# Gathering pivots in pieces, and adding the base of the formed blocks on VectorE, in a frequency-domain orthogonal convolution

## The reference

```python
x = x + conv(groupnorm(x, 32 groups))           # x is 32 x 128 x 32 x 32, float32
# conv: an orthogonal convolution, made in the frequency domain (n = 34, 34 x 18 frequencies)
V = rfft2(weight, (n, n))                        # weight 128 x 127 x 3 x 3: V is 128 x 127 per frequency
W = V^H V;  W = W + eps(frequency) * I
ortho = I - 2 * V @ solve(W, V^H)                # 128 x 128 per frequency
z = irfft2(ortho @ rfft2(pad(x)))[crop] + bias
```

## Time and profile before

| | |
|---|---|
| median of 3 runs | 3013.69 us (3006.40, 3013.69, 3032.32) |
| profiled execution | 3003.69 us, of which the span from first to last instruction is 3001.9 us |
| busy share of the span | PE 87%, DVE 64%, ACT 46%, POOL 17% |
| mean granted TensorE clock | 0.888 of full speed |

### The profile page before, as it was taken

The page is one execution under the profiler, slowest core; times in us unless marked ns, Lnnn a source line. Parts: engine busy times, 40 slices in busy tenths (PEclk is TensorE's granted clock), DMA queues, the critical chain, the costliest instruction groups (busy, mean ns, idle before and its releaser), DMA issues. The chain is left out here.

```text
span 3001.9 us, 89158 instructions
## 1 busy us (share of the span) xinstructions
PE 2597.5 (87%) x38281; PEld 2135.0 (71%) x38281; DVE 1929.9 (64%) x3842; ACT 1393.9 (46%) x3398; POOL 504.8 (17%) x872
## 2 busy tenths in 40 slices
PE   4967988998998899899796787978888899959999
PEld 4945745656566778787685766757777678959999
DVE  6844506897979768568497979788788770003333
ACT  1423424434342566666553544644556546722222
POOL 0012402131310111111110111111222223410000
PEclk7978999999998999999997978979999889967777
DMA  4283484231511366474460706241232134566662
GB/s 184 85 151 69 71 164 128 85 142 45 179 38 20 61 119 130 77 156 90 98 122 13 141 14 130 52 93 55 66 102 86 56 95 127 164 132 160 162 178 93
DMA packets 562599, 310.01 MB, mean 103 GB/s; under 512 B 484616, under 2 KB 495496, under 8 KB 561368
## 3 DMA queue, kind: packets, MB, share of 16 engines
q1 hardware_dynamic: 520896, 183.58, 29.6%
q0 software_dynamic: 41312, 120.73, 12.2%
HBM read 162.85 MB, written 141.30 MB: 101 GB/s over the span
## 5 line engine op out<-in xcount | busy, mean ns | idle before, releaser
L1390 DVE SCALAR_TENSOR_TENSOR arena<-arena,psum 128x512 f32<-128x512 f32 (+2 forms) x608 | 398.9, 719 | 310.9 <-PE psum L999 310.5
L1351 DVE TENSOR_TENSOR arena<-arena 128x960 f32<-128x960 f32 (+24 forms) x480 | 399.5, 832 | 16.6
L1346 DVE TENSOR_TENSOR arena<-arena 128x960 f32<-128x960 f32 (+8 forms) x600 | 383.0, 688 | 8.2
L978 PEld LDWEIGHTS psum<-arena 32*32 32x32 f32 x9280 | 156.2, 115 | 227.4 <-issue 216.1
L999 PE MATMUL psum<-arena 32*128 32x64 f32 x9280 | 305.3, 278 | 9.8 <-ACT arena L1163 9.8
L999 PEld LDWEIGHTS psum<-arena 32*128 32x128 f32 x9280 | 284.3, 193 | 34.1 <-ACT arena L1163 20.4
L936 PE MATMUL psum<-arena 128*32 128x256 f32 (+1 forms) x2904 | 274.9, 429 | 29.6 <-DMA arena<-plain 11.2
L978 PE MATMUL psum<-arena 32*32 32x64 f32 x9280 | 182.4, 232 | 110.2 <-DVEq L1382 97.5
L940 PE MATMUL psum<-arena 128*32 128x256 f32 (+1 forms) x3696 | 276.1, 372 | 1.6 <-issue 1.6
L1142 ACT COPY arena<-arena 32x128 f32<-32x128 f32 (+3 forms) x496 | 222.0, 448 | 26.5 <-DVE arena L1390 12.4
L1045 PE MATMUL psum<-arena 128*128 128x160 f32 x1160 | 200.6, 316 | 26.3 <-ACT arena L1203 25.9
(11 more groups left out here) (121 smaller groups left out, 4860.9 us busy)
## 6 DMA issues: line engine op xcount, KB each, us to landing
blocks<-arena POOLq DMA_DIRECT2D x145, 256.0 KB, 2.5
arena<-blocks SPq DMA_DIRECT2D x290, 128.0 KB, 2.8
kept<-arena POOLq DMA_DIRECT2D x145, 256.0 KB, 3.1
arena<-kept SPq DMA_DIRECT2D x145, 256.0 KB, 2.9
xhat<-arena SPq DMA_DIRECT2D x32, 580.0 KB, 15.0
arena<-xhat SPq DMA_DIRECT2D x580, 32.0 KB, 2.6
yhat<-arena POOLq DMA_DIRECT2D x290, 64.0 KB, 2.6
arena<-x SPq DMA_DIRECT2D x8, 2048.0 KB, 10.1
```

What stands on the lines that cost most here:

```text
L978: ins = pe.matmul(psum[0][h, L * t:L * t + L], ce[h, sj % NCE, slot + t, :], M[h, home(q) + t, c, :], start=True, stop=True)
L1346: ins = dve.tensor_tensor(pr, spread(R[:, t, :, :, j], 3, 2 * w_), both, ALU.mult)
L1351: link(dve.tensor_tensor(rest, rest, pr[:, :, h], op))
L1390: ins = dve.scalar_tensor_tensor(old, old, K["mask"][:, piv:piv + 1], upd_bank(u, c)[:, 0:L * n].rearrange("p (t n) -> p t n", n=L), ALU.m ...
```

## The change

- The job `pivot b0` moves in front of `sweep a3`. Where a pivot job stands in front of a sweep of the other group (b0 before a3, a4 before b3, b4 before a7), ACT no longer gathers ahead of that sweep: it cuts the gather into pieces of one unit (8 quads, or 6 or 7; 8 pieces for group b, 11 for group a), spreads them evenly over the units of the sweep, and does each after the `copy_ju` of the following unit, where `gather_next` stands in other sweeps.
- `pivot a0` is gathered in the same pieces too, each as soon as the form units that it reads are in `M`.
- In form a, PE leaves out the matmuls for the base. DVE instead of ACT empties the bank, with one addition of the bank and the base (`tensor_tensor`, PSUM and SBUF to SBUF). Form b is as before.
- A table's tile is loaded anew only when the units that used it are in `M`, not when PE has formed them.

```diff
@@ order()
         if k == LB - 1:
-            out.append(("form", b, 0))
+            out += [("form", b, 0), ("pivot", b, 0)]
         out.append(("sweep", a, k))
-    out.append(("pivot", b, 0))
@@ SP
-                                    sp.wait_ge(S["formed" if used == "form" else "pre_done"], end)
+                                    sp.wait_ge(S["form_copied" if used == "form" else "pre_done"], end)
@@ PE: combine(), form()
-                        for p in range(LB):
+                        for p in range(LB if with_base else 0):
                             pe.matmul(columns[quadrant(p)]..., K["ident"][:, quadrant(p)],
-                                      spread(base[:, 0:m, :], 1, n), start=alone, stop=False)
+                                      spread(base[:, 0:m, :], 1, n), start=True, stop=False)
...
-                                                coefs[:, 0:m, L * p:L * p + L], start=False, stop=alone and a == n - 1)
+                                                coefs[:, 0:m, L * p:L * p + L], start=not with_base, stop=a == n - 1 or not with_base)
...
-                        combine(tile, n, QUAD * q, columns).then_inc(S["formed"], 1)
+                        combine(tile, n, QUAD * q, columns, with_base=q >= FIRST[GROUPS[1][0]]).then_inc(S["formed"], 1)
@@ ACT
                     def gather(sj, q, n):
                         act.wait_ge(S["taken"], factor_at[g, k])
+                        if k == 0:
+                            act.wait_ge(S["form_copied"], len([f for f in form_units[:formed_by[g]] if f[0] < q + n]))
+                        elif k == LB:
+                            act.wait_ge(S["s_copied"], coupled_by[g])
...
+                    def sweep_beside(at):
+                        return at + 1 < len(jobs) and jobs[at + 1][0] == "sweep" and jobs[at + 1][1] != jobs[at][1]
...
+                    def pivot_pieces(g, k):
+                        out = []
+                        for t in GROUPS[g]:
+                            q = FIRST[t]
+                            for n in UNITS_OF_SET[t]:
+                                out.append((set_job_at[g, k, t], q, n))
+                                q += n
+                        return out
...
-                            for u in range(lo, hi):
+                            for u in range(lo, hi) if g else ():
                                 copy_form(u)
...
-                            for t in GROUPS[g]:
-                                gather(set_job_at[g, k, t], FIRST[t], SLOTS_OF[t])
+                            for piece in () if sweep_beside(at) else pivot_pieces(g, k):
+                                gather(*piece)
                         elif kind == "sweep":
                             copy_u(lo)
                             copy_ju(lo)
+                            pieces_of = pivots_beside(at)
                             for u in range(lo, hi):
                                 if u + 1 < hi:
                                     copy_u(u + 1)
                                     copy_ju(u + 1)
+                                n = len(pieces_of)
+                                for sj, q, size in pieces_of[n * (u - lo) // (hi - lo):n * (u - lo + 1) // (hi - lo)]:
+                                    gather(sj, q, size)
@@ DVE, ahead of the first factoring
+                    for u in range(formed_by[0]):
+                        q, n = form_units[u]
+                        base = tiles[load_of("form", u)[4][0]][1]
+                        dve.wait_ge(S["formed"], u + 1)
+                        dve.tensor_tensor(M[:, home(q):home(q) + n, :, :],
+                                          psum[6 + u % 2][:, 0:256 * n].rearrange("p (t c n) -> p t c n", c=QUAD, n=L),
+                                          spread(base, 1, n), ALU.add).then_inc(S["form_copied"], 1)
```

More of the change, by code:

```diff
@@ L738, in build @@
         set_job_at = {(g, k, t): n for n, (g, k, t, _) in enumerate(set_jobs)}
+        formed_by = {g: max(j[4] for j in jobs if j[0:2] == ("form", g)) for g in range(len(GROUPS))}
+        coupled_by = {g: max(j[4] for j in jobs if j[0:2] == ("mid", g)) for g in range(len(GROUPS))}
         factor_at = {j: n for n, j in enumerate(FACTOR_ORDER)}
@@ L929, in _, with combine @@
                 def _(pe):
-                    def combine(tile, units, f0, columns, alone=True):
+                    def combine(tile, units, f0, columns, with_base=True):
                         coefs, base = tile
@@ L1150, in gather_next, with pivots_beside @@
                         gather(set_job_at[g, k + 1, set_jobs[sj][2]], q, n)
+                    def sweep_beside(at):
+                        return at + 1 < len(jobs) and jobs[at + 1][0] == "sweep" and jobs[at + 1][1] != jobs[at][1]
+                    def pivots_beside(at):
+                        if at == 0 or jobs[at - 1][0] != "pivot" or not sweep_beside(at - 1):
+                            return []
+                        return pivot_pieces(*jobs[at - 1][1:3])
+                    def pivot_pieces(g, k):
[6 more added lines that the diff above has]
+                        return out
                     def copy_u(u):
```

## The result

| | before | after |
|---|---|---|
| median of 4 runs each, on one chip | 3015.93 us (3006.40 to 3032.32) | 2981.91 us (2977.84 to 2990.64) |
| profiled execution | 3003.69, span 3001.9 | 2977.84, span 2976.0 |

The ratio is 0.9884, with an interval of 0.9844 to 0.9924: 35 us less, between 23 and 47. The forecast was 2987, in a range from 2968 to 3004. The number came out; two of its terms did not, and the experiments had to find out which.

What follows compares the result with a forecast made beforehand. Waits at four pivots were taken as the bound, with table 2's landing limiting form a. Terms 13.4 + 2.1 + 8.6 - 0.5 = 23.6 off 3003.69 give 2980.1; with 7 for the runs' spread, 2987, range 2968 to 3004.

Steps and rivals of the forecast that it cites:

- Form a and pivot a0, 13.4: Start of the solver: VectorE starts factoring at 463.7 instead of 477.15, 13.4 us gained, between 12.6 and 18.3.
- six low units and one full, 11.4: Form a's seven units behind table 2: six at the low clock, one at the full, 11.4 us in all.
- The price of VectorE's addition, 0.69: Form a: VectorE's addition of bank and base, not in the trace, estimated from other rows at 0.69 us.
- room: `pre a0`, TensorE's work during the first factoring: its end keeps about 5 us to spare before it is late.
- Pivot b0, 2.1: Between sweep a3 and the mid: 2.6 us from the gather leaving, less 0.5 for pieces in a3, net 2.1.
- pivot b4: Sweep a7: the gather that goes was hidden, and the eight pieces in the sweep cost 0.5 us.
- Pivot a4, 8.6: Sweep b3: first update 11.8 us earlier, less 3.2 for its pieces, net 8.6, between 7.0 and 11.8.
- the 3.2 for two doubled units: Sweep b3: two gaps between units hold two pieces; the second piece costs 1.6 us each time, 3.2 together.
- (1): Slower rival: the clock falls in the sweeps with pieces, a3, b3 and a7; 35 us lost, 3046; 4 in 100.
- The sum: Whole kernel: 13.4 + 2.1 + 8.6 - 0.5 = 23.6 us gained of the profiled execution's 3003.69, thus 2980.1.
- Rival 2: Form a: table 2 is not late, as SyncE gets through its stores sooner; whole gain 57 us, 2953; 4 in 100.
- Rival 3: Pieces cost 0.35 us in each of the 27, 9.5 instead of 4.2 lost; about 2996; 15 in 100.

Runs made afterwards that it cites:

- A repeat: The kernel after run once more, nothing edited, on another chip against the kernel before: 0.9903, median 2993.58 us.
- the experiment with table 2: Kernel after, with form a's table 2 in a tile of its own and loaded ahead of SyncE's 16 stores: 0.9868 against the kernel before.
- the kernel with the lowest ratio: Kernel after plus table 2 loaded first, one piece per gap in sweep b3, b4 gathered ahead of a7, `pre` recut: 0.9803 against before, median 2957.04 us.
- the kernel without doubled units: Kernel after, with sweep b3's pieces spread so that no two stand between the same two units: 0.9845 against the kernel before, median 2973.06 us.
- The halves: Kernel before with only the form part (form a, pivot a0): 0.9927; with only the pieces (pivots b0, a4, b4): 0.9959.
- the kernel with a doubled unit in every sweep: Kernel without sweep b3's doubled units, with two pieces put in one gap in each of twelve sweeps: 3004.93 us, a single execution.

## Why the prediction was right, and where it was not

**Form a and pivot a0, 13.4**: right in mechanism, small in size. Table 2 bounds form a and lands when it did; seven units at the mostly low clock follow. I took six low units and one full, 11.4; they took 9.2. The last hand-overs and the last piece were as sized. The transpose came 15.3 earlier counted from the span's start, and 17.4 relative to SyncE's first table DMA, since that itself was 2.2 later and the stores took 49.50 instead of 51.86. A repeat gives 16.6. Most of it is the gather's place (11.7); the lighter units give some 3 to 4. The price of VectorE's addition, 0.69, was exact. `pre a0` kept 5.80 of room, as said; the experiment with table 2 shows that little was to be won there beyond it.

**Pivot b0, 2.1**: the mid's part came as sized (third `copy_j` 11.58 behind the last update; forecast 11.4, before 14.04). What hides it is the sweep ahead. A sweep a3 or a7 takes either 39 to 42 us or 45 to 47, by how long the low clock lasts at its start: with pieces 7 long of 13, without pieces 4 long of 7. So the pieces do not choose. Within a kind, a long sweep takes some 1.8 more with them (46.92 to 47.06, against 45.00 to 45.33). In a short one the sign is open: a7 takes 40.09 to 40.23 with them and 39.08 and 39.46 without, but a3 40.34 to 41.35 with them and 41.73 without. I had said 0.5. By the long sweeps pivot b0 is worth 2.5 less 1.8, that is 0.7, and **pivot b4** -1.8 instead of -0.5, but neither is firm. The stretch from the end of sweep a3 to sweep b0's first update takes 92.1 to 92.8 in the three profiles with the gather there and 87.2 to 92.3 in the seven without. And from the end of sweep a6 to that of a7, a short a7 takes 132.9 to 133.1 with the pieces and 133.5 and 134.2 without, a long one 141.1 to 141.4 and 140.0 to 140.3: pivot b4 is between 1.4 lost and 1.3 gained. Taking b4's gather out again was part of the kernel with the lowest ratio, but not tried alone. The 5.2 of sweep a3 in the table and most of the 7.1 of sweep a7 are each a long sweep against a short one, once in after and once in before.

**Pivot a4, 8.6**: here a step failed. "Sweep b3's first update about 6 behind its first apply" held nearly (7.52; 6.46 in the kernel without doubled units), and 10.8 came back there. But the 3.2 for two doubled units measured 5.3 to 13.1 in four profiles (35.26 to 43.07, less 29.94). I had counted the wait alone, 1.6 each, and it was 1.72 and 1.79; the clock that falls behind it was in a rival of its own, (1), at 4 in 100, and there only as a fall in all three sweeps at once. It is a term of the sum: of the eighteen such waits in these runs sixteen had a fall behind them. I wrote that no row shows a fall within a sweep, and took that for evidence that there is none. The trace of the kernel before has one, in the last unit of sweep a2 (granted clock 0.50 from 874 to 875); here behind the same matmuls of sweep a0:

```profile
604.57 1.57 PE L999 MATMUL psum<-arena 32*128 32x64 f32 x48 [0.57 <-ACT arena L1163]
...
872.36 1.93 PE L999 MATMUL psum<-arena 32*128 32x64 f32 x48 [0.57 <-ACT arena L1163]
```

And the row that I set against the rival, sweep a0's last units with 1.32 of idling, tells of VectorE's idling, not of TensorE's. Net, pivot a4 was worth 0.4 in this profile, 0.4 to 7.3 in the four with doubled units, and 12.0 with the units undoubled.

On the page that spoke against cutting gathers: the Trainium skill (VectorE: DVE Perf Modes, "The TRN2 errata") gave an estimate of 1.2 for a doubled piece, against 1.6 from the rows. TensorE's wait was 1.72, nearer to the row. On the clock, the Trainium skill (TensorE: Matmul & The Clock Gate, Part 1) has the low level as the default that activity lifts. The 0.57 behind the wait at 1478.53 agrees in that the level is low behind a pause. That TensorE was then busy for 19.47 of 20 us, most of them at the low level, is shown by these runs alone.

**The sum** was 23.6 and the profile's was 25.9, but not by the same terms: too little at the start by 2 to 4, too much at a4 by 8.2, 5.2 and 4.3 lost in sweep a3 and in b0 to b2, and 16.0 found in a7 and ahead of b7, mostly because two executions of nearly the same work ran differently. That these cancel is luck. The halves, by their medians, came to 22 (12 to 33) and 12 (3 to 22), where the terms say 13.4 and 10.2: the times alone would have refuted neither. **Rival 2** (table 2 not the bound) is out: TensorE waited 16.3 to 21.7 for it in the five profiles. **Rival 3** (0.35 a piece, 9.5 instead of 4.2 lost) is out in its mechanism: the eleven pieces of sweep b3, none doubled, cost 0.6 together, and in a long sweep eight cost 1.8, 0.23 each. But in amount its 9.5 was nearer to what the pieces took from the kernel as it is (10.4 in sweep b3 alone) than my 4.2.

## What to carry to other kernels

When small work is moved into the gaps of a loop that keeps TensorE busy, price not only the wait that it makes but the clock behind it; two pieces in one gap mostly cost 1.6 to 3.2 here, where eleven single ones cost 0.6 together, and a gap ahead of the loop's first unit is cheaper than a second piece inside. Ask of the engine that a freed resource will wait for next (here `pre a0`) how much room it has: that room bounds what the next edit can bring (5.80 here, and 3.8 came). And before a total is taken as proof, set the stretches of the two profiles side by side, for two wrong terms and some luck add up to a right number.

## What the runs showed of the hardware

- Of eighteen waits of TensorE of 1.5 to 1.8 us in otherwise dense sweeps (six in sweep b3, twelve in the kernel with a doubled unit in every sweep) sixteen were followed by a lower granted clock: mostly for some 3 us (2.08 and 1.63 where 1.13 and 0.98 are usual), three times for some 15, 17 and 25. Two waits, both of 1.73, passed without it.
- At the start of a sweep that follows a long wait the low clock lasts differently long in executions of the same instructions: sweep a3 took 46.98 and 41.35 in two runs of the kernel after, with granted clocks of 0.50 and 1.00 in its first unit.
- SyncE's 16 stores hold its queue for 49.5 to 55.0 us, without any change to them. While they run, or just behind them, TensorE stood in form a with nothing that the profile shows as its cause ("issue"), for 3.0 us in all before, for 5.8 and 10.4 in two runs of the kernel after, and for 7.4 with table 2 first, which is part of why form a ended there only at 440.
